# Experts of a routed FFN: the up product computed with the weights stationary, from a copy that VectorE makes

## What is computed

```python
x = hidden_states.reshape(-1, h)                  # 1600 x 256
route = jax.nn.sigmoid(x @ Wr + br)               # 8 experts
max_prob = jnp.max(route, axis=1, keepdims=True)
max_ind = jnp.argmax(route, axis=1)
for e in range(n_experts):
    mask = (max_ind == e)[:, None].astype(x.dtype)
    y = jax.nn.gelu(x @ W1[e], approximate=False) @ W2[e]    # 256 -> 1024 -> 256
    out = out + mask * y
out = out * max_prob
```

## Time and profile before

| what | us |
|---|---|
| median of 3 timed runs | 2338.49 (2338.36 to 2340.51) |
| the profiled execution | 2342.73 |
| its span, first to last instruction | 2341.1 |
| TensorE busy over the span | 2062.2 |
| block stage: its beginning to the last copy out of `py` | about 2133.9 to 2303.2 |

### The profile page before, as it was taken

One profiled execution on the slowest core, in us unless ns is written; L12 is line 12 of the kernel. 1 busy time (PEld: TensorE's weight loads), 2 busy tenths in 40 slices (PEclk: granted clock), 3 DMA queues, 4 the chain that ended last, 5 costly groups with the idle time before them and its releaser, 6 DMA issues. The chain is left out here.

```text
span 2341.1 us, 48582 instructions
## 1 busy us (share of the span) xinstructions
PE 2062.2 (88%) x17426; PEld 1283.4 (55%) x17427; DVE 1312.6 (56%) x3201; ACT 1121.2 (48%) x2443; POOL 516.1 (22%) x599
## 2 busy tenths in 40 slices
PE   4888888789999996799989999999999999964993
PEld 2555555546666664566545555555555555552762
DVE  4788888535555553477835555555555555541224
ACT  2777776525555551277724444544444444420110
POOL 5677677111010001266510000000000000003002
PEclk8999999769999996899989999999999999977996
DMA  5000000022110000000000000000000000044102
GB/s 167 2 2 0 0 0 2 2 70 73 68 45 24 13 7 1 1 1 0 1 13 7 7 7 6 6 6 6 6 6 12 7 6 1 1 165 169 33 29 66
DMA packets 50376, 60.85 MB, mean 26 GB/s; under 512 B 9761, under 2 KB 44886, under 8 KB 49830
## 3 DMA queue, kind: packets, MB, share of 16 engines
q1 hardware_dynamic: 47278, 53.74, 7.4%
q0 software_dynamic: 3008, 5.91, 0.8%
HBM read 51.11 MB, written 8.52 MB: 25 GB/s over the span
## 5 line engine op out<-in xcount | busy, mean ns | idle before, releaser
L2367 ACT COPY la_pT<-la_pPT 128x400 f32<-128x400 f32 x246 | 122.0, 496 | 258.0 <-PE la_pPT L2120 257.5
L2089 PE MATMUL la_side<-la_wkv,la_inT 128*128 128x512 f32 (+1 forms) x512 | 243.9, 599 | 0.0
L2077 PE MATMUL la_side<-la_inT,la_wkv 128*128 128x461 f32 x512 | 225.5, 564 | 0.9 <-ACT la_inT L2342 0.8
L2257 DVE CUSTOM_DVE_ANT_0 la_pr<-la_pS,la_mb 100x461 f32<-100x461 f32 x256 | 148.2, 636 | 130.0 <-PE la_pS L2107 130.0
L2431 POOL TENSOR_TENSOR la_xb<-io_X,la_bo 100x256 f32<-100x256 f32 x16 | 11.7, 730 | 784.2 <-DVE io_X L2246 784.2
L2358 ACT ACTIVATE la_pr<-la_pr,la_nm 100x461 f32<-100x461 f32 x256 | 172.5, 681 | 0.0
L2120 PEld LDWEIGHTS la_pPT<-io_ident,la_pr 100*128 100x128 f32 x984 | 110.5, 142 | 102.3 <-issue 97.4
L1081 DVE TENSOR_REDUCE ca_nm<-ca_pS 100x2 f32<-100x722 f32 x128 | 116.2, 908 | 90.0 <-PE ca_pS L968 88.2
L2219 DVE COPY la_v<-la_side 128x512 f32<-128x512 f32 (+1 forms) x128 | 88.3, 690 | 131.0 <-PE la_side L2089 129.6
L1153 ACT ACTIVATE ca_pr<-ca_pS,ca_nm 100x361 f32<-100x361 f32 x256 | 130.0, 561 | 64.7 <-DVE ca_nm L1081 62.8
L2120 PE MATMUL la_pPT<-io_ident,la_pr 100*128 100x100 f32 x984 | 125.9, 250 | 1.1 <-issue 1.1
(11 more groups left out here) (360 smaller groups left out, 4256.6 us busy)
## 6 DMA issues: line engine op xcount, KB each, us to landing
rf_w<-in_L_ffn_W SPq DMA_DIRECT2D x16, 1024.0 KB
ca_cn<-in_ctx SPq DMA_DIRECT2D x16, 256.0 KB
far_cn<-in_ctx SPq DMA_DIRECT2D x16, 256.0 KB
rows_in<-io_zero SPq DMA_DIRECT2D x20, 128.0 KB, 1.8
rb_xr<-rows_in POOLq DMA_DIRECT2D x20, 128.0 KB, 2.3
rows_out<-rb_yr SPq DMA_DIRECT2D x20, 128.0 KB, 1.7
ea_wcT<-in_t_L_ffn_conv_W SPq DMA_DIRECT2D x1, 2048.0 KB
la_wkv<-in_L_xattn_Wkv SPq DMA_DIRECT2D x1, 2048.0 KB
```

What stands on the lines that cost most here:

```text
L2077: last = nc.tensor.matmul(pf[:, 0:SK], wkv[:, k, e * P:(e + 1) * P], inT[:, k, :], start=k == 0, stop=k == KD - 1)
L2089: last = nc.tensor.matmul(pf[0:keys[c], :], inT[:, k, c * P:c * P + keys[c]], wkv[:, k, o:o + 512], start=k == 0, stop=k == KD - 1)
L2257: ins = nc.vector.tensor_tensor_reduce(out=pr[m % 4][:, e, 0:SK], in0=pS[0:T, 2 * (m % 2) + e, 0:SK], in1=mb[b][:, :], scale=-1.0, scalar= ...
L2367: nc.scalar.copy(pT[m % 2][:, e, :], src[:, 0:NC * T]).then_inc(s_PT, 1)
```

## The change

Up is computed with the weights stationary and the tokens moving: sixteen matmuls (eight groups of 128 hidden features, two halves of the 256 inputs) with 128 moving columns of `xT`, so that the result already lies with the hidden features on partitions. `turn_g`, `take_g`, the tile `g` and the PSUM tile `pg` go; gelu writes `gT`, which now has two buffers. The stationary operand is a copy of the block's expert in `wu` (two buffers, 128 x 2048 each), which VectorE makes in `take_w`: for block k+1 between take_x(k+1) and take_y(k-1), and for blocks 0 and 1 ahead of their take_x. VectorE reads the expert's number for it and waits for `experts_ready` and for up(k-1) to have read the buffer. TensorE waits for `up_weights_ready` in its place, and reads the number for down alone.

```diff
@@ -2624,14 +2624,15 @@
         with bk:
             xr = [bk.sb(f"xr{l}", [P, D]) for l in range(2)]
             xT = [bk.sb(f"xT{l}", [P, KD, P]) for l in range(2)]
-            g, gT = bk.sb("g", [P, F]), bk.sb("gT", [P, KF, P])
+            gT = [bk.sb(f"gT{l}", [P, KF, P]) for l in range(2)]
+            wu = [bk.sb(f"wu{l}", [P, KD, F]) for l in range(2)]
             yr = [bk.sb(f"yr{l}", [P, D]) for l in range(2)]
             px, py = bk.ps("px", [P, 512]), bk.ps("py", [P, 512])
-            ph, pg = bk.ps("ph", [P, 2, 512]), bk.ps("pg", [P, 2, 512])
+            ph = bk.ps("ph", [P, KF, P])
             s_xr = [bk.sem(f"block_loaded{l}") for l in range(2)]
             s_st = [bk.sem(f"block_stored{l}") for l in range(2)]
             s_xTp, s_xT, s_h, s_g = (bk.sem(n) for n in ("xT_in_psum", "xT_ready", "h_in_psum", "gelu_ready"))
-            s_gp, s_gT, s_y, s_yr = (bk.sem(n) for n in ("gT_in_psum", "gT_ready", "y_in_psum", "y_ready"))
+            s_y, s_yr, s_wu = (bk.sem(n) for n in ("y_in_psum", "y_ready", "up_weights_ready"))
 
             with nc.Block() as block:
                 @block.sync
@@ -2669,29 +2670,21 @@
                             last = nc.tensor.transpose(px[:, c * P:(c + 1) * P], xr[l][:, c * P:(c + 1) * P], ident[:, :])
                         last.then_inc(s_xTp, 1)
 
-                    def up(k, l, e):
-                        pe.wait_ge(s_wr, e + 1)
+                    def up(k, l):
+                        pe.wait_ge(s_wu, k + 1)
                         pe.wait_ge(s_xT, k + 1)
                         above(pe, s_g, k)
-                        for n in range(2):
+                        for f in range(KF):
                             for c in range(KD):
-                                last = nc.tensor.matmul(ph[:, n, :], xT[l][:, c, :], w1[:, e, c, n * 512:(n + 1) * 512],
+                                last = nc.tensor.matmul(ph[:, f, :], wu[l][:, c, f * P:(f + 1) * P], xT[l][:, c, :],
                                                         start=c == 0, stop=c == KD - 1)
                         last.then_inc(s_h, 1)
 
-                    def turn_g(k):
+                    def down(k, l, e):
                         pe.wait_ge(s_g, k + 1)
-                        above(pe, s_gT, k)
-                        for f in range(KF):
-                            last = nc.tensor.transpose(pg[:, f // 4, (f % 4) * P:(f % 4 + 1) * P],
-                                                       g[:, f * P:(f + 1) * P], ident[:, :])
-                        last.then_inc(s_gp, 1)
-
-                    def down(k, e):
-                        pe.wait_ge(s_gT, k + 1)
                         above(pe, s_yr, k)
                         for f in range(KF):
-                            last = nc.tensor.matmul(py[:, 0:D], gT[:, f, :], w2[:, e, f, :],
+                            last = nc.tensor.matmul(py[:, 0:D], gT[l][:, f, :], w2[:, e, f, :],
                                                     start=f == 0, stop=f == KF - 1)
                         last.then_inc(s_y, 1)
 
@@ -2701,64 +2694,67 @@
                     def two(j):
                         for m in range(2):
                             k = 2 * j + (m + 1)
-                            turn_g(k - 1)
-                            up(k, (m + 1) % 2, expert(k))
+                            up(k, (m + 1) % 2)
                             turn_x(k + 1, m % 2, j + 1)
-                            down(k - 1, expert(k - 1))
+                            down(k - 1, m % 2, expert(k - 1))
                     turn_x(0, 0, 0)
-                    up(0, 0, expert(0))
+                    up(0, 0)
                     turn_x(1, 1, 0)
                     two(0)
                     with pe.Fori(1, NBK // 2 - 1) as j:
                         two(j)
-                    turn_g(NBK - 2)
-                    up(NBK - 1, 1, expert(NBK - 1))
-                    down(NBK - 2, expert(NBK - 2))
-                    turn_g(NBK - 1)
-                    down(NBK - 1, expert(NBK - 1))
+                    up(NBK - 1, 1)
+                    down(NBK - 2, 0, expert(NBK - 2))
+                    down(NBK - 1, 1, expert(NBK - 1))
 
                 @block.scalar
                 def _(ac):
-                    def body(k):
+                    def body(k, l):
                         ac.wait_ge(s_h, k + 1)
-                        above(ac, s_gp, k)
-                        nc.scalar.activation(g[:], ph[:, :, :].rearrange("p n c -> p (n c)"), ACT.Gelu).then_inc(s_g, 1)
-                    body(0)
-                    with ac.Fori(1, NBK) as k:
-                        body(k)
+                        above(ac, s_y, k - 1)
+                        nc.scalar.activation(gT[l][:, :, :].rearrange("p f t -> p (f t)"),
+                                             ph[:, :, :].rearrange("p f t -> p (f t)"), ACT.Gelu).then_inc(s_g, 1)
+                    body(0, 0)
+                    body(1, 1)
+                    with ac.Fori(1, NBK // 2) as j:
+                        body(2 * j, 0)
+                        body(2 * j + 1, 1)
 
                 @block.vector
                 def _(dv):
+                    def expert(k):
+                        return dv.value_load(ebu[0:1, bass.ds(k, 1)], min_val=0, max_val=E - 1)
+
+                    def take_w(k, l, e):
+                        dv.wait_ge(s_wr, e + 1)
+                        above(dv, s_h, k - 1)
+                        nc.vector.tensor_copy(wu[l][:, :, :].rearrange("p k f -> p (k f)"),
+                                              w1[:, e, :, :].rearrange("p k f -> p (k f)")).then_inc(s_wu, 1)
+
                     def take_x(k, l):
                         dv.wait_ge(s_xTp, k + 1)
                         above(dv, s_h, k - 1)
                         nc.vector.tensor_copy(xT[l][:, :, :].rearrange("p k t -> p (k t)"), px[:, 0:D]).then_inc(s_xT, 1)
 
-                    def take_g(k):
-                        dv.wait_ge(s_gp, k + 1)
-                        above(dv, s_y, k)
-                        nc.vector.tensor_copy(gT[:, :, :].rearrange("p f t -> p (f t)"),
-                                              pg[:, :, :].rearrange("p n c -> p (n c)")).then_inc(s_gT, 1)
-
                     def take_y(k, l, n):
                         dv.wait_ge(s_y, k + 1)
                         above(dv, s_st[l], 16 * n)
                         nc.vector.tensor_copy(yr[l][:], py[:, 0:D]).then_inc(s_yr, 1)
 
+                    take_w(0, 0, expert(0))
                     take_x(0, 0)
+                    take_w(1, 1, expert(1))
                     take_x(1, 1)
                     def two(j):
                         for m in range(2):
                             k = 2 * j + (m + 1)
-                            take_g(k - 1)
                             take_x(k + 1, m % 2)
+                            take_w(k + 1, m % 2, expert(k + 1))
                             take_y(k - 1, m % 2, j)
                     two(0)
                     with dv.Fori(1, NBK // 2 - 1) as j:
                         two(j)
-                    take_g(NBK - 2)
                     take_y(NBK - 2, 0, NBK // 2 - 1)
-                    take_g(NBK - 1)
                     take_y(NBK - 1, 1, NBK // 2 - 1)
```

## The result

The changed kernel took 2324.58 us (median of 6 runs, 2319.06 to 2328.01), against 2338.88 for the kernel before on the same chips (6 runs). The ratio is 0.9937, interval [0.9921, 0.9953]: faster by 0.63%, some 14.7 us, with 11 to 18.5 inside the interval. The forecast was 2323.0 and 15.5 us less.

What follows compares the result with a forecast made beforehand. TensorE's stream, busy 88% of the span, was taken as the bound. Terms of -16.6, -1.7 and +2.8 gave -15.5 us, from 2338.49 to 2323.0, with an 8-in-10 range of 2320 to 2330.

Steps and rivals of the forecast that it cites:

- The turns: Turns of g on TensorE's path, removed for blocks 0 to 18: 0.87 us a block, 16.6 us saved.
- Up: Up product as 32 records a block, 0.112 us apart: 3.58 us instead of 3.44, 2.8 us added over 20 blocks.
- the fourth rival: Inside up, weight load and stream run in series: 0.22 us a record, up 7.04, time 2392; chance 0.03.
- The copy: VectorE's copy of up's weights during down: 1.23 us, starting 1.15 after down starts, 0.9 us to spare, costing nothing.
- The end: Block 19, ahead of the last down: 0.77 us after down 18's stream instead of 2.44, saving 1.67 us.
- The start: Ahead of the first up: early weight copies cost nothing, and TensorE's dropped number reads and addresses save nothing.
- The sequencer: TensorE's number read and addresses for down: 0.6 us read, hidden by about 2.0 us of look-ahead.
- The sum: Whole kernel: 16.6 and 1.7 us saved, 2.8 us added, together 15.5 us less.

## Why the prediction was right

- **The turns** were priced at 0.87 a block, 16.6 us for 19. The block took 7.98 before and 7.25 after, and putting eight turns back made it 8.12: 0.87 each time.
- **Up** was priced at 3.58 and took 3.57. The step that could have failed was the choice of 0.112 a record from a row with other moving columns; with half the columns the pace stayed 0.112. Weight loads and streams overlapped: the records stood 0.112 apart, where a single load of up lasted 0.19 (190 to 192 ns, the 32 of the block at 2178.66). Load and stream in series, at 0.22 a record, the fourth rival, are out by that.
- **The copy** was priced at 1.23 and took 1.23 (1.24 on average); its start was put 1.15 after that of down and came at 1.19; the copy ends at 2.42, 0.14 passes until up can start (2204.56 to 2204.70 with two copies), and up is wanted at 3.46, so 0.9 us is in hand, which the kernel with two copies confirms (up 0.23 late for 1.14 more). What the prediction did not see is the first weight load, which begins 0.2 ahead of up. A copy that ends too late for it should cost up to 0.1 even before the 0.9 is used up; that is an estimate from the kernel with two copies, and no run stands in between.
- **The end**: the gap ahead of the last down was put at 0.77 and came out 0.87. The stream of down 18 is over at 2276.63 + 3.46 = 2280.09, and down 19 starts at 2280.96. The copy out of `py` ends at 2280.70, and the release took 0.26, not 0.15. This term was mis-sized by 0.1 us; why the release took longer than in the earlier trace rows is open.
- **The start**: the first up began 4.19 us into the stage instead of 4.37; this 0.2 was not counted. Before, TensorE's sequencer computed an address after the last wait (2138.17, and the weight load followed at 2138.27); after, the load follows the wait directly. So the reads and addresses that went were not quite "nothing", but only in the first block. GpSimd's issues beside the first two copies took longer (1.76 for the first two and 1.52 for the third, where they took 1.20 and 0.54 before the change); that fell on the loads of blocks 1 and 2, where nobody waited for it.
- **The sequencer** was said to look about 2.0 us ahead of down. The read began 1.9 us ahead (2180.78 for the down at 2182.66), and after what it needs 1.04 us is in hand, by the kernel with three more reads.
- **The sum**, by the stage: 15.5 forecast, 15.8 measured; the differences are about 0.2 at the start, 0.1 in up (2.7 instead of 2.8) and 0.1 the other way at the end. By the timed medians 14.3, with an interval that holds both.

## What to carry to other kernels

A product whose result has to be turned for the next one can be computed turned: here the turns went, 0.87 us a block, and what was paid was up's time at the pace of its weight loads over its time before, 3.57 for 3.44, 0.13 us. Price that from a row with the same width of weights: past weights of 128 columns an f32 record cost 0.112 with 128 moving columns, 0.112 with 64 and 0.111 with 100. A copy of the chosen weights a block ahead was free here, on VectorE and on ScalarE, because each had room for it within the other product (1.23 and 1.89 us, in down's 3.46). On VectorE this is its length, 0.57 us ahead of it for reading the number and computing the address (2183.28 to 2183.85), and some 0.35 behind it: 0.14 for the release and 0.2 for the first weight load, which starts ahead of up. Whether the stationary operand could be taken by register from where the weights lie was not tried; the kernel with expert 0 for all shows that leaving the copy out would gain nothing.

## What was not expected

- VectorE's copy held GpSimd's DMA issues at the start of the stage: in the changed kernel the issue at 2135.90 takes 1.52 and ends at 2137.42, 0.12 after the copy (2136.07 + 1.23), where it takes 0.54 without one. The second of the two issues at 2132.14 ends the same 0.12 after the first copy (2133.90 against 2132.50 + 1.28). But in the steady block an issue that begins 0.36 us ahead of the copy (2183.49 and 2183.85) still takes 0.54, and so do those of two early blocks that begin 0.27 and 0.26 ahead (2147.26 and 2147.53, 2154.51 and 2154.77), where the copy takes 1.30 instead of 1.23; the stretched one at 2135.90 began 0.17 ahead.
- The block stage began anywhere from 2119.4 to 2133.9 us in the profiles of kernels that share all code ahead of it. That spread, 14.5 us, is nearly as large as the gain, so the length of the stage in a trace tells more than one time of the whole program.
- The first block took 6.7 to 6.95 us from turn to turn in some profiles and 7.6 in others (the twice copied, the three reads, the two PSUM tiles). The windows of up 0, in the changed kernel and in the one with two PSUM tiles:

```profile
2135.81:2141.20 5.39, 5.39 (x32) 5.39 (x33) 1.23 (x1) 0.00 (x0) 1.52 (x1) 0.66 0.07 24
2132.67:2138.99 6.32, 6.32 (x33) 6.32 (x34) 1.23 (x1) 0.00 (x0) 1.51 (x1) 0.56 0.07 21
```

The granted clock is 0.66 in the one and 0.56 in the other over the same product: it rose from 0.50 to 1.00 later. In the changed kernel it was 0.50 until 2139, 3.2 us into the product, 0.76 from there to 2140 and 1.00 after; with two PSUM tiles it was 0.50 until 2138, 5.3 us into it, and 0.86 from there to 2139. In the 40 us before, TensorE was busy 1.86 and 1.87 us, at 0.50 in both. Why it rose later in three of the profiles is open.
